# A decoder layer on one core: the first expert layer streams its weights past stationary tokens, and its sums are copied and transposed back

## The reference

```python
x = x + attn(layernorm(x), w_q, w_k, w_v)                 # 16 x 128 tokens of 256, causal, rotary
x = x + xattn(layernorm(x), ctx, Wq, bq, ..., Wc, bc)     # 8 heads, dilated windows
t = layernorm(x).reshape(2048, 256)
logits = silu(t @ rw1 + rb1) @ rw2 + rb2                  # router, 8 experts
w = softmax(top-2 of logits)                              # weight 0 for the other six
eh = silu(einsum('td,edh->teh', t, ew1) + eb1)            # layer one: 256 -> 512
eo = einsum('teh,ehd->ted', eh, ew2) + eb2                # layer two: 512 -> 256
x = x + t + einsum('te,ted->td', w, eo)
```

## Time and profile before

| what | value |
|---|---|
| median of 3 runs | 536.65 us (537.2, 531.6, 536.65) |
| profiled execution, span | 532.3 us |
| busy: PE, DVE, ACT, POOL | 475.2, 355.5, 275.6, 168.9 us |
| mean granted TensorE clock | 0.984 |
| first product of layer one, last product of layer two | 349.4 us, 518.3 us |

### The profile page before, as it was taken

The page is one execution under the profiler, slowest core; times in us unless marked ns, Lnnn a source line. Parts: engine busy times, 40 slices in busy tenths (PEclk is TensorE's granted clock), DMA queues, the critical chain, the costliest instruction groups (busy, mean ns, idle before and its releaser), DMA issues.

```text
span 532.3 us, 11817 instructions
## 1 busy us (share of the span) xinstructions
PE 475.2 (89%) x3812; PEld 336.0 (63%) x3812; DVE 355.5 (67%) x837; ACT 275.6 (52%) x715; POOL 168.9 (32%) x184
## 2 busy tenths in 40 slices
PE   6899899999999999999999998979878787878780
PEld 2455489655689755579765577958656565656560
DVE  5744766887766896776786979876685534343457
ACT  5364575266475266466356646466464545454550
POOL 1320242212033122033041123434555353535341
PEclk9999999999999999999999999999999999898996
DMA  8801000324300315300314341811322361112635
GB/s 334 325 0 41 0 2 1 120 76 163 119 0 0 118 39 197 119 0 1 113 45 158 101 186 63 337 43 53 103 62 67 97 226 48 54 57 63 218 127 214
DMA packets 20413, 54.41 MB, mean 102 GB/s; under 512 B 3365, under 2 KB 9774, under 8 KB 19600
## 3 DMA queue, kind: packets, MB, share of 16 engines
q1 hardware_dynamic: 16336, 43.32, 22.9%
q0 software_dynamic: 3744, 9.47, 6.0%
q10 hardware_dynamic: 288, 1.05, 0.6%
HBM read 36.98 MB, written 17.76 MB: 103 GB/s over the span
## 4 chain that ended last, share of the span: by engine, by line
PE 39%; issue 20%; DVE 12%; another core or an unknown queue 11%; ACT 9%; POOL 4%; ACTq 2%; DMA 1%; DVEq 0%; POOLq 0%; SPq 0%
PE pj L1458 14%; PE op L1694 6%; ACT up_f L727 5%; PE pj L1673 4%; PE sc L1650 2%; ACT up_f L517 2%; ACT up_f L733 2%; POOL pn L456 2%; PE pj L1776 1%; POOL rstd L426 1%; PE sc L1545 1%; DVE stats L764 1%; ACTq L724 1%; DVE rope L933 1%
## 5 line engine op out<-in xcount | busy, mean ns | idle before, releaser
L1458 PE MATMUL pj<-up,up_f 128*128 128x512 f16 x480 | 107.9, 379 | 4.7 <-DVE rope L934 1.9
L1458 PEld LDWEIGHTS pj<-up,up_f 128*128 128x128 f16 x480 | 45.8, 98 | 60.0 <-DVE rope L934 6.1
L676 ACT ACTIVATE p<-sc,nm 128x128 f32<-128x128 f32 x128 | 45.4, 369 | 39.2 <-DVE nm L1297 39.0
L474 POOL DMA_INDIRECT cst<-rows,src_row x39 | 42.0, 1077 | 68.5 <-DVE up_f L1224 56.0
L456 POOL TENSOR_TENSOR pn<-p,inv 128x256 f32<-128x256 f32 x64 | 37.9, 614 | 80.4 <-DVE inv L1256 80.4
L1776 PE MATMUL pj<-up_f,up 128*128 128x128 f16 x624 | 55.0, 220 | 4.9 <-issue 4.8
L1776 PEld LDWEIGHTS pj<-up_f,up 128*128 x624 | 43.3, 97 | 20.0 <-issue 9.0
L727 ACT ACTIVATE up_f<-pj,halved 128x128 f32<-128x128 f32 x104 | 29.7, 370 | 49.9 <-remote 35.6
L487 POOL DMA_INDIRECT picked<-wch,dst_row x39 | 41.2, 1056 | 22.3 <-DVE up_f L1224 9.7
L548 ACT ACTIVATE down<-pj,bias 128x512 f32<-128x512 f32 x48 | 32.5, 686 | 26.4 <-PE pj L1458 25.9
L426 POOL TENSOR_TENSOR rstd<-veps,nhalf 128x4 f32<-128x4 f32 (+1 forms) x13 | 12.7, 975 | 103.5 <-DVE veps L772 103.2
(11 more groups left out here) (272 smaller groups left out, 1025.6 us busy)
## 6 DMA issues: line engine op xcount, KB each, us to landing
raws<-in_staged SPq DMA_DIRECT2D x12, 512.0 KB, 5.3
split<-halved SPq DMA_DIRECT2D x12, 512.0 KB, 3.8
down<-split SPq DMA_DIRECT2D x4, 1024.0 KB
rows<-row SPq DMA_DIRECT2D x4, 528.0 KB, 3.1
small<-in_x SPq DMA_DIRECT2D x4, 512.0 KB, 3.7
up<-in_ctx SPq DMA_DIRECT2D x4, 512.0 KB, 4.7
v<-in_w SPq DMA_DIRECT2D x2, 1024.0 KB, 9.0
resid<-outs SPq DMA_DIRECT2D x4, 512.0 KB, 2.9
```

What stands on the lines that cost most here:

```text
L474: pool.indirect_dma_start(got[s], None, rows[0:known * L], bass.IndirectOffsetOnAxis(src_row[:, t:t + 1], 0), bounds_check=known * L - 1, ...
L676: last = act.activation(p2[:, s, i, :], sc[s][:, i * P:(i + 1) * P], ACT.Exp, bias=nm2[:, s, i:i + 1], scale=1.0, accum_out=sum2[:, s, i:i ...
L1458: last = pe.matmul(out, w(c), v(c), start=(i == 0), stop=(i == len(terms) - 1))
```

## The change

Layer one changes its roles. The tokens (`xt`, 128x128) are held stationary and 512 columns of weights move past them: 6 products of 512 columns instead of 24 of 128. The sums come out with tokens on partitions, so they have to be turned before the bias per hidden feature and the Silu. DVE copies the bank to SBUF in float32 (`keep_hidden`, into `pre`), PE transposes it back in four float32 128x128 transposes (`turn_hidden`, into the banks `ht`), and ACT's `silu` reads `ht`. Layer two is a block of its own and runs three steps behind (`LAG` = 3). The order in a PE step is layer one of `t`, `turn_hidden(t - 1)`, layer two of `t - 3`, `turn(t + 2)`. ACT runs `silu` one step later. DVE's order becomes `weigh_out(t - 4)`, `take(t + 2)`, `hidden_low(t - 2)`, `keep_hidden(t)`. `TRAIL` becomes 8, `scatter` no longer waits for `h_lo`, the banks become two each of `hb`, `ht` and `yb`, the gates eight.

```diff
-LAG = 2
+LAG = 3
-TRAIL = 2 * LAG + SLOTS
+TRAIL = 2 * LAG + 2
+GATES = 8
+BANKS = 2
...
-        hT = [room.grid(MC, P) for _ in range(SLOTS)]
+        hT = [room.grid(MC, P) for _ in range(BANKS)]
...
+        pre = [p2[:, k].rearrange("p a b -> p (a b)") for k in range(BANKS)]
...
-        tp, hb, yb = sc0, (pj0, pj1, op), (sc1, tpA, tpB)
+        tp, hb, ht, yb = sc0, (pj0, pj1), (op, sc1), (tpA, tpB)
...
-                if t + LAG + 1 < TILES:
-                    pool.wait_ge(h_lo, t + LAG + 1)
                 pool.wait_ge(y_free, t + 2)
...
             def silu(t):
-                s = t % SLOTS
-                if t >= SLOTS:
-                    act.wait_ge(h_lo, t - SLOTS + 1)
+                k = t % BANKS
+                if t >= BANKS:
+                    act.wait_ge(h_lo, t - BANKS + 1)
...
-                act.wait_ge(h_full, t + 1)
+                act.wait_ge(ht_full, t + 1)
                 for m in range(MC):
-                    last = act.activation(hT[s][:, m, :], hb[s][:, m * P:(m + 1) * P], ACT.Silu,
+                    last = act.activation(hT[k][:, m, :], ht[k][:, m * P:(m + 1) * P], ACT.Silu,
...
-            for t in range(TILES):
-                silu(t)
+            for t in range(TILES + 1):
+                if t > 0:
+                    silu(t - 1)
...
+            def keep_hidden(t):
+                dve.wait_ge(h_full, t + 1)
+                dve.tensor_copy(pre[t % BANKS], hb[t % BANKS][:]).then_inc(h_kept, 1)
...
-            for t in range(TILES + LAG):
+            for t in range(TILES + LAG + 1):
+                if t >= LAG + 1:
+                    weigh_out(t - LAG - 1)
                 if t + 2 < TILES:
                     take(t + 2)
-                if t >= LAG:
-                    weigh_out(t - LAG)
                 if t == 0:
                     rows_low_half(1)
+                if 2 <= t < TILES + 2:
+                    hidden_low(t - 2)
                 if t < TILES:
-                    hidden_low(t)
+                    keep_hidden(t)
...
+            def first_layer(t, e):
+
+                b = hb[t % BANKS]
                 if t < 1 or t == TILES - 1:
                     pe.wait_ge(tp_free, t + 1)
+                for c in range(KC):
+                    for i, (w, x) in enumerate(((0, c), (0, KC + c), (1, c))):
+                        ins = pe.matmul(b[:], xt[t % SLOTS][:, x, :], up_chunks[:, bass.ds(e * MC + 2 * c, 2), w, :],
+                                        start=(c == 0 and i == 0), stop=(c == KC - 1 and i == 2))
+                ins.then_inc(h_full, 1)
+
+            def turn_hidden(t):
+
+                k = t % BANKS
+                pe.wait_ge(h_kept, t + 1)
                 for m in range(MC):
+                    ins = pe.transpose(ht[k][:, m * P:(m + 1) * P], pre[k][:, m * P:(m + 1) * P], ident)
+                ins.then_inc(ht_full, 1)
+
+            def second_layer(t, e):
+
+                q, y = t % SLOTS, yb[t % BANKS]
+                pe.wait_ge(h_lo, t + 1)
+                for m in range(MC):
+                    at = e * (2 * MC * D) + m * 2 * D
+                    pe.matmul(y[:], hTh[q][:, m, :], down_rows[:, bass.ds(at, 2 * D)],
                               start=(m == 0), stop=False, skip_group_check=True)
+                    pe.matmul(y[:, 0:D], hTl[q][:, m, :], down_rows[:, bass.ds(at, D)],
                               start=False, stop=False, skip_group_check=True)
+                pe.matmul(y[:, 0:D], pick[:, bass.ds(e * P, P)], b2, start=False, stop=True,
+                          skip_group_check=True).then_inc(y_full, 1)
...
+                if t < TILES:
+                    first_layer(t, own[k])
+                if t == 1:
                     pe.wait_ge(op_free, OP * G)
                     pe.wait_ge(sc_free[1], SC[1] * (G - 1) + 4)
+                if 1 <= t <= TILES:
+                    turn_hidden(t - 1)
...
+                if t >= LAG:
...
+                    second_layer(t - LAG, (own if same else before)[old])
```

More of the change, by code:

```diff
@@ L277, in decoder @@
         beforeh, onesh, iotah = (sb(n, [P, P], F16) for n in ("beforeh", "onesh", "iotah"))
-        gate = [sb(f"gate{s}", [P, 1]) for s in range(STEPS)]
+        gate = [sb(f"gate{s}", [P, 1]) for s in range(GATES)]
+        pre = [p2[:, k].rearrange("p a b -> p (a b)") for k in range(BANKS)]
         src_row, dst_row = sb("src_row", [P, TILES], U32), sb("dst_row", [P, TILES], U32)
@@ L294, in decoder @@
         tp_full, tp_free, gated = sem("tp_full"), sem("tp_free"), sem("gated")
-        h_full, silu_done, h_hi, h_lo = (sem(n) for n in ("h_full", "silu_done", "h_hi", "h_lo"))
+        h_full, h_kept, ht_full, silu_done, h_hi, h_lo = (
+            sem(n) for n in ("h_full", "h_kept", "ht_full", "silu_done", "h_hi", "h_lo"))
         y_full, y_free, y_part = sem("y_full"), sem("y_free"), sem("y_part")
@@ L732, in silu @@
                     act.wait_ge(y_full, t - SLOTS + 1)
-                act.activation(hTh[s][:], hT[s][:], ACT.Copy, scale=MID).then_inc(h_hi, 1)
+                act.activation(hTh[t % SLOTS][:], hT[k][:], ACT.Copy, scale=MID).then_inc(h_hi, 1)
             act.wait_ge(row_out, 16 * (G - 1) + 16)
@@ L1223, in hidden_low @@
                 dve.wait_ge(h_hi, t + 1)
-                dve.scalar_tensor_tensor(out=hTl[s][:], in0=hT[s][:], scalar=MID, in1=hTh[s][:], op0=ALU.mult,
+                dve.scalar_tensor_tensor(out=hTl[s][:], in0=hT[t % BANKS][:], scalar=MID, in1=hTh[s][:], op0=ALU.mult,
                                          op1=ALU.subtract).then_inc(h_lo, 1)
+            def keep_hidden(t):
+                dve.wait_ge(h_full, t + 1)
+                dve.tensor_copy(pre[t % BANKS], hb[t % BANKS][:]).then_inc(h_kept, 1)
             def take(t):
@@ L1233, in take @@
                 dve.wait_ge(gathered[s], 16 * (t // SLOTS + 1))
-                if t >= STEPS:
-                    dve.wait_ge(y_free, t - STEPS + 2)
-                dve.tensor_scalar(gate[t % STEPS][:], got[s].bitcast(F32)[:, bass.ds(e + D, 1)], MID_DOWN, None,
+                if t >= GATES:
+                    dve.wait_ge(y_free, t - GATES + 2)
+                dve.tensor_scalar(gate[t % GATES][:], got[s].bitcast(F32)[:, bass.ds(e + D, 1)], MID_DOWN, None,
                                   ALU.mult).then_inc(gated, 1)
@@ L1243, in weigh_out @@
                 dve.wait_ge(y_full, t + 1)
-                g = gate[t % STEPS]
-                dve.tensor_scalar(ys[s], yb[s][:, 0:D], g[:], None, ALU.mult).then_inc(y_part, 1)
+                g, y = gate[t % GATES], yb[t % BANKS]
+                dve.tensor_scalar(ys[s], y[:, 0:D], g[:], None, ALU.mult).then_inc(y_part, 1)
                 dve.wait_ge(y_part, t + 1)
-                dve.scalar_tensor_tensor(out=ys[s], in0=yb[s][:, D:2 * D], scalar=g[:], in1=ys[s],
+                dve.scalar_tensor_tensor(out=ys[s], in0=y[:, D:2 * D], scalar=g[:], in1=ys[s],
                                          op0=ALU.mult, op1=ALU.add).then_inc(y_free, 1)
@@ L1752, in _ @@
             down_rows = down[:].rearrange("p e m k d -> p (e m k d)")
-            up_rows = up[:].rearrange("p e m k d -> p (e m k d)")
             next_turn = ctx.enter_context(pe.register("next_turn"))
@@ L1764, in experts @@
                 return [(w >> (3 * k)) & (E - 1) for k in range(STEPS)]
-            def step(t, e, before):
-                s, q = t % SLOTS, (t - LAG) % SLOTS
+            up_chunks = up[:].rearrange("p e m k d -> p (e m) k d")
+            def first_layer(t, e):
+                b = hb[t % BANKS]
                 if t < 1 or t == TILES - 1:
                     pe.wait_ge(tp_free, t + 1)
-                for m in range(MC):
[L1772 to L1787, removed]
@@ L1788, in step @@
+            def second_layer(t, e):
[4 more added lines that the diff above has]
+                    pe.matmul(y[:], hTh[q][:, m, :], down_rows[:, bass.ds(at, 2 * D)],
                               start=(m == 0), stop=False, skip_group_check=True)
-                    pe.matmul(yb[q][:, 0:D], hTl[q][:, m, :], down_rows[:, bass.ds(at, D)],
+                    pe.matmul(y[:, 0:D], hTl[q][:, m, :], down_rows[:, bass.ds(at, D)],
@@ L1790, in step @@
                               start=False, stop=False, skip_group_check=True)
-                if before is not None:
-                    pe.matmul(yb[q][:, 0:D], pick[:, bass.ds(before * P, P)], b2, start=False, stop=True,
-                              skip_group_check=True).then_inc(y_full, 1)
+                pe.matmul(y[:, 0:D], pick[:, bass.ds(e * P, P)], b2, start=False, stop=True,
+                          skip_group_check=True).then_inc(y_full, 1)
             pe.wait_ge(sc_free[0], SC[0] * (G - 1) + 5)
@@ L1808, in _ @@
                     before, own = own, experts()
-                if t == LAG:
+                if t < TILES:
+                    first_layer(t, own[k])
+                if t == 1:
                     pe.wait_ge(op_free, OP * G)
```

(10 more changed lines are left out.)

## The result

The changed kernel takes 517.9 us (median; 517.1 to 518.7) against 536.85 us before: ratio 0.966, 95% interval 0.963 to 0.969. The forecast was 515, range 505 to 530. The span of the profiled execution is 516.9 us, 15.4 less than the 532.3 before. The medians differ by 19. The profiled execution before was one of the quick ones of its kernel, so I account for the span and read the gain from the ratio.

The account below looks back on a forecast made before the run. No engine was full in the late tiles; late PE signals and the order of waits bound them. Late -19.5, middle -3, start 0, end +0.6 sum to -21.9 us: 536.65 becomes 514.8, rounded 515, range 505 to 530.

Parts of the forecast that it names:

- The late stretch: Tiles 15 to 38: dense steps of 3.5 us, 80.5 us in place of 100.0, a gain of 19.5.
- the longer cover: Slack between PE's signals and their use: 1.0 us before, 2.5 or more after; 3 us lateness then costs 0.4.
- dense step of 3.36: Late tiles of the kernel before: a PE step without gap takes 3.36 us, every second step being late.
- rival 1: Late tiles: signals stay late every second step, pitch 4.05 us, time 529; chance 0.14.
- The cause of the late signals: Late tiles: PE's signals some 3 us late, taken as tied to POOL's back-to-back indirect transfers.
- The middle stretch: Tiles 4 to 15: 44.6 us against 47.9, a gain of 3, bounds 0 and 9.
- the 0.5 us a step for gaps: Tiles 4 to 15: gaps between DVE's small chained operations, 5.5 us on top of 39.1 busy.
- cover of 2.5 us: PE's wait for DVE's copy: asked for 3.5 us after layer one ends, so 2.5 us or more to spare.
- The end: After tile 38's step begins: the way to its weighing grows from 7.1 to 7.7 us, a loss of 0.6.
- The start: Tiles 0 to 4: DVE's first copy stands behind the last rows' low part; put at 0, bounds -1 to +2.
- rival 3: Late tiles: transposes not counting as busy PE halve the clock, +61 us, near 598; chance 0.02.
- Rival 2: `turn_hidden`: PE waits for the copy behind DVE's in-order queue, 4.8 us a tile, time 550; chance 0.07.

Follow-up runs that it names:

- E7: The changed kernel with the four float32 transposes done twice per tile: 525.5 us, ratio 0.983.
- E1: The kernel before with only the scatters' wait for a later tile's low part removed: 536.1 us, ratio 1.000.
- E2: The kernel before with layer two three steps behind instead of two and the scatters' wait removed: 539.0 us, ratio 1.006.
- E3: The changed kernel with layer one cut to 24 products of 128 columns in place of 6, tokens still stationary: 536.9 us, ratio 1.001.
- E9: The changed kernel with 24 products of 128 columns and without the scatters of tiles 17 to 38: 521.2 us, ratio 0.972.
- E5: The kernel before without the scatters of tiles 17 to 38 and without the scatters' wait: 515.5 us, ratio 0.964.
- E10: The changed kernel without the scatters of tiles 17 to 38: 513.6 us, ratio 0.958.
- E4: The changed kernel with layer two two steps behind instead of three, and a wait keeping two banks: 544.8 us, ratio 1.018.
- E6: The changed kernel with DVE's copy of layer one's sums made twice per tile: 523.6 us, ratio 0.981.
- E8: The changed kernel with the copy moved from DVE to ACT for every tile: 511.4 us, ratio 0.958.

## Why the prediction was right, and where not

**The late stretch: right in size, and half right in cause.** The forecast was 23 x 3.5 = 80.5 us; it is 80.5. That agrees partly by luck: dense steps are 3.37, near the lower bound of 3.35, and seven longer ones, six of 3.6 to 3.8 and one of 4.4, make up the rest. E7 shows that PE's products are the bound there, and that transposes cost 0.11 us each. But the prediction named the longer cover and the removed wait as what takes the stalls away. E1 shows that the removed wait bunches nothing, and E2 that the longer lag on top of it gains nothing. What it takes is fewer and longer products: E3 undoes only that and loses everything. Of the rise in pitch of 0.91 (4.38 - 3.47) the seams explain 0.05 us a tile, and E9 shows that the rest goes when POOL is relieved. The prediction's base was off as well: its dense step of 3.36 was already held up, since E5 takes 3.0 to 3.1 for the same work. So the new step of 3.37 is some 0.3 us more work for PE, and the gain, but for the little that the clock has in it, is that PE is no longer held; the sum of the streams, 3.35, was the right way to price it. Of the arguments, "fewer instructions on PE" stood only as one against rival 1, unpriced. It was the main one.

**The cause of the late signals.** The prediction tied them to POOL's bursts and said that the rows only show the two together. E5 shows that they are a cause. With E3 and E10 it shows that they are one of two factors: bursts with few PE instructions, or dense PE instructions with few transfers, cost little. E4, E6 and E7 point at the bursts, as the prediction had it, and not at the number of transfers: in pairs, as many made no signal late. No run changes the grouping alone. E1 shows POOL waiting for a take that a late signal held up, so burst and lateness may feed each other; which comes first is open.

**Rival 1** expected the late signals to stay and cost 0.4 us of wait and 0.7 of holes a pair. The signals did stay in part and the holes did not, so the price came out near 0.1 us a tile (3.47 against the 3.38 of E10). Two signs that the prediction named for being wrong did appear, POOL back to back and, in the middle, PE waiting for the copy, and ACT waited for "remote" up to 2.1 us where under 1 was forecast; the time came out in range even so, because short waits of this kind cost PE little here.

**The middle stretch: the term was mis-sized.** Forecast -3, measured -0.2. The 47.9 us that it started from were 45.6 between the true ends. DVE's busy time was foreseen well, 39.1 against 39.96 us. The step that failed is the 0.5 us a step for gaps. With the copy in line PE now has to wait for it, 5.3 us in all. The prediction had that only as a cover of 2.5 us, worked out for late tiles; in the middle the sorting uses that cover up. E6 and E8 show it from both sides: one copy more costs 0.45 us a tile there, one copy less gives 0.40.

**The end: mis-sized.** Forecast +0.6, measured +2.9. The prediction left out that the low part stands behind the weighing, and the weighing behind a scatter of an earlier tile, 1.59 us in the row above. Its cuts also overlap: the late stretch ends with tile 38's layer one, and the end's 7.1 us begin with it. Counted from the end of that layer one, its own working is 4.5 us before and 6.4 after, a loss of 1.9 and not 0.6, and 8.6 were measured.

**The sum.** In the span the forecast was -21.9 and -15.4 was measured, 6.5 us less: the middle and the end, with the overlap, are nearly all of it. That 515 still lies within 3 us of 517.9 is half luck: the forecast added 4.35 us from span to time, because the profiled execution before was a quick one; after, the median stands 1.0 over the span.

**The start** was put at 0 and the end of tile 4's layer one moved by 0.2 us, although the clock was granted at 0.90 in that stretch (0.53 from 349.4 to 353.0, mostly the half level), where it was 1.00 before.

**The clock (rival 3)** did not happen: the late stretch, with eight transposes a tile (four float32, four float16), has 1.00. By the rule of the Trainium skill, TensorE: Matmul & The Clock Gate, Part 4: PE-mode transpose, transposes don't count as a busy PE in the same way; twelve transposes a tile in E7 had 1.00 from 414 to 498 us as well, so the rule had no consequence here.

**Rival 2** (slower, PE held by DVE's queue) has a relative in E4: 1.8% slower with one step less of distance. But there PE waits for the low part and not for the copy, and its signals are on time, so the lateness that the rival was built on has no part in it.

## What to carry to other kernels

Where an engine with many short matrix products runs beside a steady stream of indirect transfers from GpSimd, count PE's instructions, not only its columns: the same columns in a quarter of the products took the holes away. Look also at how the transfers are grouped: late signals stood beside four in a row and, in E4, E6 and E7, not beside pairs with rest between. When work is moved to another engine to relieve the bound, look at that engine's load in every stretch, not on average: the copy was free for 23 tiles and cost the possible gain in 11, and ACT had the room. When two variants differ in several things, test each alone: the removed wait and the longer lag gain nothing without the new roles, and the new roles lose without the lag. And take the price of a part from an undisturbed stretch: the seams looked like 0.47 us a tile in E3 and are 0.05 in E9.

## What the runs showed of the hardware that was not expected

Signals of PE arrive up to 3.7 us after the product that carries them when two things coincide: dense short products and four indirect transfers of POOL in a row, 0.3 us apart. With long products and four in a row they are up to 2.7 us late (the changed kernel). With 22 or 23 transfers in 50 us PE issued 806 to 911 products and loads and had holes of 0.4 to 0.5 us with no wait shown; with 17 transfers it issued 1061 to 1107. With 25 to 30 transfers, all or nearly all in pairs (E4, E6, E7, all with long products), no signal was late. Short products beside transfers in pairs were not tried. DVE's signals weren't looked at for this. What holds PE's signals was not found; the runs show only the two factors. Each time here comes with a record of the instructions, so whether recording them has a part in it was not told apart either.
